# Where residual, statistics and masks of an eight-layer program are made: the reshaped attention, the first norm and the linear stage

## What is computed

```python
x = x + _layernorm(_L0_attn_ref(_layernorm(x), Wq, Wk, Wv))
x = x + _layernorm(_L0_ffn_ref(_layernorm(x), ...))
...                       # test-time learner, switch layer
x = x + _layernorm(_L2_attn_ref(_layernorm(x), W_qkv))
...                       # expert choice, rotary attention, elastic mixture
```

```python
out = jnp.einsum('hbqk,hbkd->hbqd', atten, V).reshape(b, s, -1)
y = out + x
mu = jnp.mean(y, axis=(1, 2), keepdims=True)
var = jnp.var(y, axis=(1, 2), keepdims=True)
return (y - mu) / jnp.sqrt(var + EPS)
```

## Time and profile before

| | us |
|---|---|
| median of three runs (lowest to highest) | 1970.25 (1969.66 to 1971.28) |
| the profiled execution | 1970.37 |
| its span in the trace | 1968.5 |

### The profile page before, as it was taken

The page is one execution under the profiler, slowest core; times in us unless marked ns, Lnnn a source line. Parts: engine busy times, 40 slices in busy tenths (PEclk is TensorE's granted clock), DMA queues, the critical chain, the costliest instruction groups (busy, mean ns, idle before and its releaser), DMA issues. The chain is left out here.

```text
span 1968.5 us, 25704 instructions
## 1 busy us (share of the span) xinstructions
PE 1537.5 (78%) x8391; PEld 810.1 (41%) x8391; DVE 1236.7 (63%) x2890; ACT 1024.0 (52%) x2001; POOL 788.0 (40%) x1500
## 2 busy tenths in 40 slices
PE   2799999994459880636761793599999999899997
PEld 1133333321347770525661562123333333477776
DVE  3688888884755532026648642978888888354553
ACT  2377777774523430217643321167777777555543
POOL 3455555423534535046523585514444441111220
PEclk9699999997566665767755897589999999999999
DMA  4122222200000004100006133211111111100000
GB/s 118 69 66 66 66 66 65 66 27 1 1 2 1 1 1 125 36 23 4 2 0 174 29 41 61 75 37 61 66 60 60 62 64 44 46 2 10 12 12 11
DMA packets 84969, 85.16 MB, mean 43 GB/s; under 512 B 35942, under 2 KB 67536, under 8 KB 84708
## 3 DMA queue, kind: packets, MB, share of 16 engines
q1 hardware_dynamic: 73914, 75.14, 12.0%
q0 software_dynamic: 7680, 6.06, 2.0%
q10 hardware_dynamic: 3242, 2.32, 0.4%
HBM read 59.76 MB, written 25.17 MB: 43 GB/s over the span
## 5 line engine op out<-in xcount | busy, mean ns | idle before, releaser
L937 DVE TENSOR_REDUCE arena<-psum 128x2 f32<-128x1024 f32 x512 | 601.7, 1217 | 105.1 <-PE psum L730 99.5
L842 ACT ACTIVATE arena<-psum 128x512 f32<-128x512 f32 x1024 | 553.8, 595 | 138.9 <-PE psum L743 130.3
L730 PE MATMUL psum<-arena 72*128 72x512 bf16 x1024 | 288.0, 397 | 46.6 <-DMA arena<-L_k_parts 17.3
L743 PE MATMUL psum<-arena 99*128 99x512 bf16 x1024 | 311.9, 386 | 11.4 <-issue 7.6
L753 PE MATMUL psum<-arena 128*32 128x512 f32 x2048 | 274.5, 608 | 3.0 <-ACT arena L842 1.9
L2460 POOL TENSOR_SCALAR arena<-arena 128x4 f32<-128x4 f32 x112 | 31.2, 279 | 413.9 <-DVE arena L2454 409.3
L743 PEld LDWEIGHTS psum<-arena 99*128 99x128 bf16 x1024 | 74.6, 98 | 288.0 <-ACT arena L842 222.9
L730 PEld LDWEIGHTS psum<-arena 72*128 72x128 bf16 x1024 | 95.4, 99 | 190.5 <-DVE arena L937 29.0
L2489 ACT ACTIVATE arena<-arena 128x128 f32<-128x128 f32 x208 | 85.3, 481 | 130.8 <-POOL arena L2466 113.3
L2451 DVE BATCH_NORM_STATS2 arena<-arena 128x6 f32<-128x128 f32 x448 | 96.5, 277 | 57.1 <-PEq L101 21.2
L636 POOL TENSOR_TENSOR arena<-arena 128x16 bf16<-128x16 f32 x64 | 14.3, 223 | 292.5 <-DVE arena L937 220.2
(11 more groups left out here) (434 smaller groups left out, 2430.6 us busy)
## 6 DMA issues: line engine op xcount, KB each, us to landing
arena<-L_q_parts SPq DMA_DIRECT2D x192, 96.0 KB
arena<-L_k_parts SPq DMA_DIRECT2D x180, 96.0 KB
L_q_parts<-arena SPq DMA_DIRECT2D x16, 384.0 KB, 3.3
L_k_parts<-arena SPq DMA_DIRECT2D x16, 384.0 KB, 3.2
arena<-in_L_ffn_w SPq DMA_DIRECT2D x1, 2048.0 KB
ec_result<-arena SPq DMA_DIRECT2D x1, 2048.0 KB, 9.7
arena<-in_L_ffn_fc2s SPq DMA_DIRECT2D x1, 2048.0 KB, 18.0
ec_normed<-arena SPq DMA_DIRECT2D x2, 1024.0 KB, 7.8
```

Source lines behind the costliest of these rows:

```text
L730: last = nc.tensor.matmul(bank[:, 512 * h:512 * h + 512], columns(q9[0:QK_ROWS], i, m // 2, 128 * (2 * (m % 2) + h), 128), columns(k9[0:QK ...
L743: nc.tensor.matmul(acts.bank(name), columns(k9[0:ROWS], i, g, 128 * k, 128), columns(q9[0:ROWS], i, g, 0, 512), start=True, stop=True).the ...
L842: nc.scalar.activation(prob[:, k % 2, g, :], acts.bank(name), ACT.Exp, scale=scale).then_inc(act_taken, 1)
L937: nc.vector.tensor_reduce(neg_max[:, i % 2, 2 * m:2 * m + 2], maxes.bank(("max", i, m)).rearrange("p (h t) -> p h t", h=2), axis=AX.X, op= ...
```

## The change

It has three parts, and a fourth that follows from them. (1) In the first attention DVE adds n to the finished tile (`add_tokens`, k=2), takes its statistics (`token_stats`, k=3) and sums them up (`token_spread`, k=0 of the next quad). (2) `norms` gives way to `first_norm`: no residual and no statistics of o; factors of batch 0 and of batches 1 to 7; DVE adds the scaled o to x, ACT no longer applies factors to o and copies to `nT` in DVE's place; the product of shift and scale is left to `c.late`, which the learner's stage now sums in two steps. (3) In the linear stage GpSimd's fetch stands behind `of_x4.factors`, ACT's `of_x5.apply` behind `soften`, and the mask at the head of a round. (4) The stages now take 7, 41, 22, 11, 70, 20, 61, 47, 57 and 43 semaphores, so that clears come behind the channel mix (at 82), the switch layer (90), the expert choice (108) and the mixture, at the program's end (100).

```diff
@@ first_norm, in place of norms
+            dve.wait_ge(means_summed, 1)
+            ch.next(nc.vector.tensor_reduce(mean, of_batches(sums[:, 0:TILES]), axis=AX.X, op=ALU.add))
...
+            def add(b):
+                dve.wait_ge(o_fact, 1 if b == 0 else 2)
                 for t in range(TPB * b, TPB * b + TPB):
+                    nc.vector.scalar_tensor_tensor(c.x[:, t, :], c.o[:, t, :], of_o.scale[:, t:t + 1], c.x[:, t, :],
+                                                   op0=ALU.mult, op1=ALU.add).then_inc(added, 1)
+
+            add(0)
+            for b in range(B):
+                if b + 1 < B:
+                    add(b + 1)
+                dve.wait_ge(added, TPB * (b + 1))
+                of_x.spread(dve, c.x, b)
...
+            pool.wait_ge(batch_var, 1)
+            ch.next(nc.gpsimd.tensor_tensor(rs, var, c.minus_half[:, 0:B], ALU.pow))
+            ch.next(nc.gpsimd.tensor_tensor(rs2, rs, rs, ALU.mult))
+            factors(0, 1)
+            factors(1, B)
+            of_x.factors(pool, 0)
+            pool.wait_ge(o_fact, 2)
+            nc.gpsimd.tensor_tensor(c.late, of_o.shift, of_o.scale, ALU.mult)
+            for b in range(1, B):
+                of_x.factors(pool, b)
...
+            nc.tensor.matmul(sums[:, 0:TILES], c.ones, c.mv[:, :, 0], start=True, stop=True).then_inc(means_summed, 1)
...
+            for b in range(B + 1):
+                if b < B:
+                    of_x.apply(act, c.n, c.x, b)
+                if b >= 1:
+                    act.wait_ge(turned, b)
+                    nc.scalar.activation(c.nT[:, b - 1, 1:S + 1], c.bank((b - 1) % 2), ACT.Copy).then_inc(copied, 1)
@@ attention_layer, DVE
+            def add_tokens(i):
+                dve.wait_ge(o_done, i + 1)
+                nc.vector.tensor_tensor(c.o[:, i, :], c.o[:, i, :], c.n[:, i, :], ALU.add).then_inc(residual, 1)
+
+            def token_stats(i):
+                dve.wait_ge(residual, i + 1)
+                nc.vector.bn_stats(c.stats[:, i, :], c.o[:, i, :]).then_inc(y_stats, 1)
+
+            def token_spread(i):
+                dve.wait_ge(y_stats, i + 1)
+                nc.vector.bn_aggr(c.mv[:, i, :], c.stats[:, i, :]).then_inc(y_mv, 1)
...
+                    if by_tokens and k == 2 and i >= 1:
+                        add_tokens(i - 1)
+                    if by_tokens and k == 3 and i >= 1:
+                        token_stats(i - 1)
+                    if by_tokens and k == 0 and i >= 2:
+                        token_spread(i - 2)
...
             normalise(LAST)
+            if by_tokens:
+                token_spread(LAST - 1)
+                add_tokens(LAST)
+                token_stats(LAST)
+                token_spread(LAST)
@@ test_time_learner, GpSimd
-            nc.gpsimd.tensor_tensor(c.late, of_o2.shift, of_o3.shift, ALU.add).then_inc(late_summed, 1)
+            nc.gpsimd.tensor_tensor(c.late, c.late, of_o2.shift, ALU.add).then_inc(late_summed, 1)
+            pool.wait_ge(late_summed, 1)
+            nc.gpsimd.tensor_tensor(c.late, c.late, of_o3.shift, ALU.add).then_inc(late_summed, 1)
@@ linear_layer: GpSimd, ACT, DVE
+                if inside(i):
+                    of_x4.factors(pool, i)
                 if inside(i + FETCH_AHEAD):
                     fetch(pool, i + FETCH_AHEAD, fetched[i + FETCH_AHEAD])
-                if inside(i):
-                    of_x4.factors(pool, i)
...
                     soften(i - 2)
+                if inside(i - 4):
+                    of_x5.apply(act, c.n, c.x, i - 4)
                 if inside(i - 1):
                     copy(i - 1)
                 if inside(i - 2):
                     turn(i - 2)
                 if inside(i - 4):
-                    of_x5.apply(act, c.n, c.x, i - 4)
                     copy_tokens(i - 4, turned5, copied5)
...
             for i in range(LAST_ROUND):
+                if inside(i - 3):
+                    mask(i - 3)
                 if inside(i - 2):
                     scale(i - 2)
...
-                if inside(i - 2):
-                    mask(i - 2)
```

More of the change, by code:

```diff
@@ L235, in _ @@
[L235 to L247 removed]
+            ch = Chain(dve, dve_step)
@@ L295, in _ @@
[L295 to L310 removed]
+                ch.next(nc.gpsimd.tensor_tensor(of_batches(full[:, at]), of_batches(c.mv[:, at, 1]), wide(rs2), ALU.mult))
@@ L2841, in program @@
         stage(reshaped_attention)
-        stage(norms, "norm1", after_layer=True, scale_of_batch=True)
+        stage(first_norm)
         stage(channel_mix, d)
```

201 lines of the change are left out of this document (34 added, 167 removed).

## The result

| | us |
|---|---|
| changed kernel, median of four runs (lowest to highest) | 1949.6 (1948.46 to 1951.25) |
| kernel before, median of four runs | 1970.76 |
| ratio | 0.9892, 95% interval 0.987 to 0.9914 |
| profiled execution of the changed kernel, its span | 1951.25, 1949.5 |

The change makes the kernel 21 us faster (17 to 26 by the interval), where 16 were forecast. The forecast's range began at 1949.5: the median lies on that bound, and the ratio times the 1970.25 on which the forecast was made is 1949.0, half a microsecond outside. Six more runs, beside eleven of the kernel before, gave nearly the same ratio, 0.9883 (0.9852 to 0.9915).

What follows compares the result with a forecast made beforehand. No engine bounds the whole: PE paces the first attention, the first norm is a chain, the linear stage a loop. 1970.37 − 11.6 (norm, attention's 0.9 included) − 5.0 (linear) + 0.75 (clears) = 1954.5 us; range 1949.5 to 1962.

Steps and rivals of the forecast that it cites:

- part 3: Linear stage: moved fetch and ACT applications gain 3.0 us at the start, 0 in steady rounds, 2.0 at the end; −5.0 together.
- Attention: Three DVE operations per quad, 0.73 us, covered by DVE's waits and a margin: 0 for the steady quads.
- Rival (a): Attention insertions partly on the path, 0.1 to 0.3 us a quad, 3 to 9 in all: 1957 to 1963; chance 0.20.
- (d): DVE becomes the attention's limit, all 23.4 us on the path: 1978, slower than before; chance 0.03 with over 0.6 a quad.
- the margin of 0.29 behind 283.35: Attention, first pair of takes: room before PE's second score tile needs the freed bank, more than BN_AGGR's 0.16 us.
- End of the attention: Behind the last division nothing covers the last two tiles' operations, 0.89 us; the norm's first instruction comes +0.9, at 471.98.
- First norm: Sums start at 472.0, one block of 28 columns, then DVE 2.37 us a batch; ends at 509.8 instead of 521.42, 11.6 earlier.
- Start of the linear stage: Factors of x of batch 0 no longer stand behind four fetch DMAs: 3.0 us earlier.
- Rival (b): Linear stage: DMAs ahead of the factors of o cost 3 to 5 us, the start's gain: 1957.5 to 1959.5; chance 0.13.
- End of the linear stage: Batch 7's logarithm starts earlier, kv, mask and turn follow 2.2 earlier; last output waits for the mask, 2.0 us earlier.
- Clears: Semaphore clears between stages: three old ones cost 3.37 us, four new ones 4.12, so +0.75 if the program's end counts.
- Rival (c): More gain: the end's clear outside the time (−1.06), clock and rounds by 2 better, 1949 to 1952; chance 0.10.

Runs made afterwards that it cites:

- apply_only: Kernel before with ACT's applications of x of batch i-4 moved ahead of the copies in the linear stage, nothing else; stage 178.12 us, ratio 0.9976.
- fetch_only: Kernel before with GpSimd's fetch behind the factors of x in every round of the linear stage, nothing else; stage 180.27 us, ratio 0.9996.
- apply_of_batch_5: Kernel before with ACT's applications moved in round 9 alone, batch 5 ahead of the copy of qT of batch 7; stage 181.81 us.

## Why the prediction was wrong in a size, and right in most of its mechanism

The kernel came out faster than forecast by 5 us, just beyond the range. The step that failed is the end of the linear stage in part 3: the prediction let the last output wait for a mask whose end it kept from the old trace, and kept the old durations of PE's rows with it, 2.0 us; apply_only measured 5.3. The rest held, with smaller errors.

**Attention: right, with a price too high that nothing depended on.** PE busy all the time, the whole unchanged to 0.01 us, as forecast, and the earlier trace rows gave the reason: operations placed in waits of 0.75 and 0.48. The forecast added durations (0.73 a quad, DVE at 303). The rows overlap their neighbours' ends, and what the three cost is what they take from the waits, 0.21, 0.20 and some 0.06; DVE is at 294.40 (and 26 quads lie in the window, not 28). All 32 adds took 0.27 to 0.29, but only seven of them had a GpSimd operation beside them, six of these a copy in SBUF. In those seven the rule of the Trainium skill (SBUF — State Buffer, Who interferes with whom) that the prediction weighed did not show (0.28 and 0.29); for the other 25 no run here tests it. Rival (a) is out, and (d) too as an account of this kernel; but (d)'s mechanism is real one place further on. The same three operations in the first quarter cost 16.5 us in the attention and, by the totals, all of the change's gain, and the row that foretold it was the margin of 0.29 behind 283.35, not DVE's share of 87%.

**End of the attention.** The tail took 0.87 (0.89 forecast). The norm came at 471.26 and not 471.98 because the first quad of this execution was 0.66 us early, before anything that the change touches.

**First norm: right, 1.1 us too long.** Start at the first sum, one block with a power of 4.82, all later work behind DVE. The mis-sized term is the batch: 2.37 us, from 571.65 to 574.02, where DVE had just come out of a wait; in a row of such batches each takes 2.22. Seven of them are 1.0.

**Start of the linear stage: right.** −3.0 forecast, −3.15 in the changed kernel and −3.14 in fetch_only, which keeps 2.9 in its one trace. The steady rounds cost 0: DVE's add of o ended 1.0 us before the values (42.01 and 42.99 us behind the stage's start for batch 2), as worked forward. Rival (b) is out. The decay to 1.7 in the changed kernel is no sign of it, since the same kernel, run again, had 3.9 at that batch.

**End of the linear stage: this is the term that failed.** Forecast 2.0, and it is 5.3 in apply_only and in the changed kernel (31.79 before, 26.50 in both). The step was "the last output waits for the mask, which ends at 1012.89, and starts at 1012.95 instead of 1014.91". That wait did change hands as said, worth 1.97 (apply_of_batch_5 shows it alone). But the mask's end was taken from the trace as fixed, though I had just moved what comes ahead of it. In the trace of before it hangs on two ends that meet. DVE's scaling of batch 7 ends at 1005.27, PE's output of batch 6 at 1005.21, and the division behind both (L1955) opens the row that ends with the mask (L1947 and the two behind it):

```profile
1004.04 1.23 DVE L1977 TENSOR_TENSOR arena<-arena 128x1024 f32<-128x1024 f32 x1 [2.67 <-ACT arena L1895]
1005.25 0.56 DVE L1955 RECIPROCAL arena<-psum 128x64 f32<-128x64 f32 x1
...
1012.30 0.13 DVE L1947 TENSOR_SCALAR arena<-psum 128x1 f32<-128x1 f32 x1
```

The earlier logarithm, forecast as 2.2, brought the scaling 2.4 us forward. And the eight rows of the output, at 1.2 GHz before, ran at 2.4, 1.74 us shorter; the mask came as much earlier. By these ends neither alone would have moved the division by more than 0.1 us. Then the last output also ran at the higher clock, 1.57 shorter. 1.96 + 1.74 + 1.57 = 5.27. The prediction named the clock as what could change the stage, with ±2, and gave it no direction. Why the clock follows the order of work here stays open; that it does, and what it gives, is shown.

**Clears: right.** 0.97, 1.00, 1.16 and 1.08 for the new ones where 0.95, 1.00, 1.11 and 1.06 were forecast; 1.41, 0.97 and 1.11 for the old where 1.36, 0.94 and 1.07 were. Sum +0.72 beside +0.75.

**The rest.** Linear 2.0 and norm with its start 1.8 make the trace 3.8 shorter than forecast; the stages that nobody touched were 0.7 longer, and this profiled execution was 1.7 over the median of its four. How much of the 21 us is the linear stage is known to some 3 us only, by the spread of its traces. Rival (c) came nearest, for its "clock and rounds" and not for the end's clear, which counts in the trace.

## What to carry to other kernels

Put small operations where their engine waits for the busiest one and ask of each place how long the wait is: the same 0.8 us of work costs nothing in two waits and 0.55 us a quad one quarter further. Where a step moves, follow everything behind it once more, instead of taking the next event's end from the old trace. Of a DMA issue that is moved behind one chain, look at what it now runs into: moved in one round only, it met the next round's and lost half of the gain there. And compare a stage with itself before comparing it with another: two traces of one kernel differed here by 2.2 us in a stage of 176.

## What the runs showed of the hardware

- The granted clock of PE in the short stretches of the linear stage is not the same between executions of the same instructions: the output of batch 0 took 2.08 us in one of the changed kernel and 3.78 in another, and the stage's length moved by 1.2 us in the old stage (183.19 to 184.42) and by 2.2 in the new one (174.00 to 176.23). At the end of the stage it follows the order of work in each of 15 traces. PE's wait ahead of an output doesn't predict it (2.80 us at one level, 2.81 and 1.22 at the other). The Trainium skill (TensorE: Matmul & The Clock Gate, What's actually happening) says that the count of slow matmuls at a kernel's start varies from run to run. No run here was read for its start; inside the kernel the output of batch 0 varies in the same way, and that of batch 6, the same in all traces of one order, does not.
- Three BN_STATS of 128x128, each 0.28 us in the trace, start 0.19 to 0.20 us apart when they stand in a row.
- A power on GpSimd costs 0.15 to 0.16 us a column over a base of 0.4: 1.04 for 4 columns, 1.64 for 8, 3.56 for 20, 4.82 for 28.
